# Four-head score pieces in the context attention of a two-layer decoder kernel

## The chip, the cores and the metric

The kernel runs on one core of a Trainium2 chip. The metric is the device time of one execution in microseconds (us), from its start to its end, as the median of several executions. The profile records one execution with a start and an end for every instruction. Its span runs from the first recorded instruction to the last.

## What is computed

The reference is a pre-norm decoder over x of shape (32, 112, 256), with two layers of causal attention, attention over a context and a mixture of experts. The change touches only the context attention of the second layer, which is cut here to what matters:

```
xn = layernorm(x)                       # 32 batches, 112 rows, 256 wide
q = rope(heads(xn @ Wq))                # 16 heads of 16
k = rope(heads(ctx @ Wk))               # ctx: 375 rows of a batch
v = heads(ctx @ Wv)
p = softmax(q @ k.T / 4)                # per head 112 x 375
x = x + (p @ v) @ Wo + bo
```

## The kernel before

**Stages.** The kernel runs its phases one after another. The context attention (class ContextAttention, from L1916, run by `stream`, L699) is one of them: in the trace its score matmuls run from 1754 us to 2398 us. It is one software pipeline over frames. In frame e every named piece works on batch e minus its age, so that one frame holds work of up to six batches. With 32 batches and ages of 0 to 5 there are 37 frames, and in 27 of them (5 to 31) every piece is present. The order of the pieces in a frame is one list written by hand (L1924), and all engines walk it in this order, each doing its part of a piece. Each engine works strictly in this order, so an engine that waits holds up all that it has behind the waiting piece. The trip through the frames is unrolled by 12.

**PSUM.** Six of the eight banks hold scores, as three pairs, 0, 1 and 2. The other two form a ring (class Ring, L226): each piece that isn't in the `bankless` list claims the next of the two in turn, and TensorE waits in `claim` until the piece that used this bank two claims earlier has been emptied by its reader.

**The pieces of one batch.** `stats` and `scale` normalise x on VectorE, with one power on GpSimd in between. `ctx0`, `ctx1` and `xT` transpose the context and x on TensorE, and ScalarE copies each out of its ring bank. `q`, `k0` and `k1` project, and ScalarE copies the results to `kq_raw`. Behind the last of the three in the frame's order ScalarE issues two transfers that exchange the halves of the partitions (`exchange`, L2151, to `kq_swapped`). `rope` on VectorE is three operations of 128x974 (L2207, L2210, L2211), the second of which waits for the exchange. Then 16 transfers issued by SyncE (`place_half`, L1992) spread the result to `slots`: each head lies in a 32-row slot, four heads side by side on the 128 partitions, four such groups g. `v0` to `v2` project the values.

**The scores.** A score piece is made for one group g and one half of its four heads: `g0` to `g3` for the first two heads, `h0` to `h3` for the other two. TensorE runs two matmuls of 32x112 by 32x375, each on its own 32 rows of the array and into its own bank of one pair (L2036; the trace records two instructions for each fp32 matmul, so x4 is one piece of two heads). VectorE takes the maximum over the 375 columns of both banks in one operation (L2194). After the last maximum VectorE writes the negative maxima to `top_wide` (L2203); `put` transposes them on TensorE (L2043), and VectorE adds them to q (L2215), so that the scores that are made a second time, transposed, come out with the maximum taken off. `tr0` to `tr2` (L2056) make these: sixteen matmuls of 32x125 by 32x112 each, on four row groups, into four banks (two pairs). One exponential of 125x1792 on ScalarE (L2141) empties them. `headsA` and `headsB` (L2095) multiply by the values, `back0`, `back1` (L2104) transpose back, VectorE divides (L2222, L2225), `onT` (L2111) transposes, `project` (L1563) projects and VectorE adds to x (L1587).

**Which pair serves which piece** is `first_pair` (L1932). `bank_free` (L2162) makes TensorE wait, before it writes a pair, for the reader of the piece that used it last: the maximum for a `g` or `h` piece, the exponential for a `tr` piece. The old order:

```
h0 g0 headsB tr0 g1 q back0 tr1 k1 k0 stats scale back1 h1 g2 onT rope
v0 ctx0 tr2 v1 xT h2 g3 h3 ctx1 headsA v2 project put
```

rope, stats and scale have no part on TensorE. `Ring.filled` and `Ring.freed` count the banks, and `copy_out` (L929) is the ScalarE copy whose line in the trace is L932.

Of the kernel before, what the change touches and what calls it, by code (L numbers as in the profile page):

```python
# [27 lines left out]
ALU = mybir.AluOpType  # L28
# [3 lines left out]
T = 112  # L32
# [7 lines left out]
S2 = 375  # L40
# [1875 lines left out]
class ContextAttention(Streamed):  # L1916
# [4 lines left out]

    def __init__(self, nc, G, W):
        super().__init__(nc, G, W)
        self.plan = Flow(2, [("h0", 3), ("g0", 3), ("headsB", 5), ("tr0", 4), ("g1", 3), ("q", 1), ("back0", 5),  # L1924
# [3 lines left out]
                             ("project", 5), ("put", 3)],  # L1928
                         bankless=("tr0", "tr1", "tr2", "g0", "h0", "g1", "h1", "g2", "h2", "g3", "h3", "rope", "stats", "scale"),
                         ahead=8, behind=5, turns=3, unroll=12)  # L1930

        self.first_pair = {"g0": 0, "g1": 0, "g2": 2, "g3": 1, "h0": 1, "h1": 0, "h2": 2, "h3": 0,  # L1932
                           "tr0": 1, "tr1": 0, "tr2": 0}
        names = [name for name in self.plan.names if name in self.first_pair]
        self.score_names = names
        self.last_maximum = [name for name in names if name[0] in "gh"][-1]
        self.last_raw = [name for name in self.plan.names if name in ("q", "k0", "k1")][-1]

    def allocate(self, sb, sem):
        self.norm = self.allocate_norm(sb, sem)  # L1940
        self.allocate_end(sb, sem)
        N = self.plan.turns
        self.ctx = self.G["contexts"]
        self.ctxT = [sb(f"ctxT{i}", [P, DC, S2]) for i in range(N)]
        self.xn, self.xT = sb("xn", [P, D]), sb("xT", [P, DC, T])
        self.kq_raw, self.kq_swapped = sb("kq_raw", [P, DC, KQ]), sb("kq_swapped", [P, DC, KQ])
        self.kq_part, self.kq = sb("kq_part", [P, DC, KQ]), sb("kq", [P, DC, KQ])
        self.slots = [sb(f"slots{i}", [P, HG, KQ]) for i in range(N)]
# [7 lines left out]
        self.scored, self.maxed = [sem(f"scored{i}") for i in range(2)], [sem(f"maxed{i}") for i in range(2)]  # L1956
# [66 lines left out]
    def pe(self, pe, name, b, par, c, body):  # L2023
        nc, ring, W = self.nc, self.ring, self.W
        slots = self.slots[par]
        if name in ("g0", "g1", "g2", "g3", "h0", "h1", "h2", "h3"):

            g, half = int(name[1]), "gh".index(name[0])
            if name == self.score_names[[n[0] in "gh" for n in self.score_names].index(True)]:
                pe.wait_ge(self.slotted, 256 * (b + 1))  # L2030
                self.tiles_set_up(pe, b)
            self.bank_free(pe, name, b)
            for a in range(2 * half, 2 * half + 2):
                slot = slice(SLOT * a, SLOT * (a + 1))
                at = 512 * (2 * self.first_pair[name] + a % 2)
                ins = nc.tensor.matmul(self.scores[0:T, at:at + S2], slots[slot, g, S2:KQ], slots[slot, g, 0:S2],  # L2036
                                       start=True, stop=True)
            ins.then_inc(self.scored[half], 1)
        elif name == "put":
            bank = ring.claim(pe, c, body)  # L2040
            pe.wait_ge(self.wide_ready, b + 1)
# [4 lines left out]
        elif name[0:2] == "tr":  # L2046
# [5 lines left out]
            for g in range(HG):  # L2052
                for a in range(HS):
                    slot = slice(SLOT * a, SLOT * (a + 1))
                    at = 512 * (2 * self.first_pair[name] + a) + g * T
# [62 lines left out]
    def act(self, act, name, b, par, c, body):  # L2118
        if name in ("ctx0", "ctx1"):
            self.copy_out(act, c, body, self.ctxT[par][:, int(name[3]), :], lambda bank: bank[:, 0:S2])  # L2120
        elif name == "xT":
            self.copy_out(act, c, body, self.xT[:].rearrange("p f t -> p (f t)"), lambda bank: bank[:, 0:DC * T])
        elif name == "q":
            at_least(act, self.turned, b)
            self.copy_out(act, c, body, self.kq_raw[:, :, S2:KQ], lambda bank: bank[:, 0:DC * T].rearrange("p (g t) -> p g t", g=DC))
            self.exchange(act, name, b)
        elif name in ("k0", "k1"):
            at_least(act, self.turned, b)
            self.copy_out(act, c, body, self.kq_raw[:, int(name[1]), 0:S2], lambda bank: bank[:, 0:S2])
            self.exchange(act, name, b)  # L2130
        elif name in ("v0", "v1", "v2"):
            self.tiles_set_up(act, b)
            self.copy_out(act, c, body, self.v[par][0:CK, int(name[1]), :, 0:HD],
                          lambda bank: bank[0:CK, 0:D].rearrange("t (h d) -> t h d", h=H))
        elif name[0:2] == "tr":
            i = int(name[2])
            act.wait_ge(self.flipped_ready, b * CC + i + 1)
            if i == 0:
                self.reuse(act, "headsB", b)
            at = 1024 * self.first_pair[name]  # L2140
            self.nc.scalar.activation(self.probsT[0:CK, i, :, :],  # L2141
                                      self.scores[0:CK, at:at + 2048].rearrange("t (a c) -> t a c", c=512)[:, :, 0:HG * T], ACT.Exp,
                                      scale=self.scale).then_inc(self.exped, 1)
        elif name in ("headsA", "headsB"):
            first = 0 if name == "headsA" else 2
            self.reuse(act, "back1" if first else "back0", b)
            self.copy_out(act, c, body, self.heads_raw[:, first * T:(first + 2) * T], lambda bank: bank[:, 0:2 * T])
        elif name == "onT":
            self.act_onT(act, b, c, body)
# [8 lines left out]
    def pairs_of(self, name):  # L2158
        first = self.first_pair[name]
        return {first, first + 1} if name[0] == "t" else {first}  # L2160

    def bank_free(self, pe, name, b):  # L2162
        names, age = self.score_names, self.plan.age
        here = names.index(name)
        waits = {}
        for pair in self.pairs_of(name):
            for back in range(1, 2 * len(names)):
                frame, at = divmod(here - back, len(names))
                other = names[at]
                if pair not in self.pairs_of(other):  # L2170
# [4 lines left out]
                i = int(other[-1])  # L2175
                sem, per = (self.exped, CC) if other[0] == "t" else (self.maxed["gh".index(other[0])], HG)
                waits[other] = (sem, before * per + i + 1)
                break
        for sem, count in waits.values():
            pe.wait_ge(sem, count)  # L2180
# [1 line left out]
    def dve(self, dve, name, b, par, c, body, chain):  # L2182
# [3 lines left out]
        elif name == "scale":  # L2186
            self.reuse(dve, "xT", b)
            self.norm_scale(dve, self.norm, b, self.xn[0:T, :], X[0:T, b, :]).then_inc(self.xn_ready, 1)
            nc.vector.tensor_tensor(X[0:T, b, :], X[0:T, b, :], self.W["cb"][0:T, :], ALU.add).then_inc(self.x_biased, 1)
        elif name in ("g0", "g1", "g2", "g3", "h0", "h1", "h2", "h3"):  # L2190
            g, half = int(name[1]), "gh".index(name[0])
            dve.wait_ge(self.scored[half], b * HG + g + 1)
            at = 1024 * self.first_pair[name]
# [1193 lines left out]
```

## Time and profile before

| | |
|---|---|
| median of 3 executions | 3161.06 us (3157.9 to 3165.23) |
| the profiled execution | 3160.0 us |
| its span | 3158.1 us |
| TensorE busy | 2782.6 us, 88% |
| VectorE busy | 2276.4 us, 72% |
| ScalarE busy | 1662.1 us, 53% |
| GpSimd busy | 961.8 us, 30% |
| mean granted TensorE clock | 0.939 |

PE is TensorE's matmuls, PEld its weight loads (which overlap them), DVE is VectorE, ACT ScalarE, POOL GpSimd and SP SyncE. The share of busy time is over the whole span; what counts for a change in one phase is the state of the engines in that phase. A clock of 1.00 is the upper of TensorE's two levels, 2.4 GHz, and 0.50 the lower, 1.2 GHz.

### The profile page before, as it was taken

What the parts mean: (1) busy time and instruction counts of PE and PEld (TensorE: products, weight loads), DVE (VectorE), ACT (ScalarE), POOL (GpSimd) and SP (SyncE); (2) the same over time, 40 slices, a digit from 0 to 9 for tenths busy, and PEclk for the clock granted to TensorE, in tenths of its full rate; (3) what the DMA queues carried; (4) which work ended last, traced back from release to release, by engine and by line L of the source; (5) the groups of instructions that cost most, each with busy time, mean ns of one, the idle gap of its engine ahead of it and who ended that gap; (6) DMA issues with size and microseconds to landing.
All of it is one profiled execution on the core that took longest, in us unless ns stands there. A gap on an engine that the chain in (4) does not pass through costs nothing. (4 is left out here: it accounts for less than half of the span.)

```text
span 3158.1 us, 76055 instructions
## 1 busy us (share of the span) xinstructions
PE 2782.6 (88%) x28240; PEld 2034.1 (64%) x28240; DVE 2276.4 (72%) x4894; ACT 1662.1 (53%) x3243; POOL 961.8 (30%) x1219
## 2 busy tenths in 40 slices
PE   7999899999999999667998799999997999983980
PEld 6887466666666665555886466666665777763970
DVE  5998567777777776567887577767763899984756
ACT  4777455655655555343554244444443788862540
POOL 0000344554555555460000100000000134546771
PEclk9999999999999999688999799999997999996995
DMA  7930354455445444262000333333330777857758
GB/s 179 300 92 0 109 158 141 132 162 162 139 146 165 150 132 152 86 203 72 0 0 7 63 71 71 72 71 72 72 62 22 232 230 231 247 173 219 225 173 249
DMA packets 364789, 413.72 MB, mean 131 GB/s; under 512 B 108017, under 2 KB 330513, under 8 KB 364369
## 3 DMA queue, kind: packets, MB, share of 16 engines
q1 hardware_dynamic: 218176, 220.63, 26.1%
q10 hardware_dynamic: 127216, 139.94, 15.1%
q0 software_dynamic: 19104, 49.22, 4.5%
q8 instruction: 189, 3.10, 0.4%
q14 instruction: 104, 0.84, 0.1%
HBM read 125.33 MB, written 252.45 MB: 120 GB/s over the span
## 5 line engine op out<-in xcount | busy, mean ns | idle before, releaser
L814 POOL TENSOR_TENSOR x_rstd<-x_var,g_minus_half 112x1 f32<-112x1 f32 x128 | 74.8, 585 | 710.5 <-DVE x_var L810 709.9
L2194 DVE TENSOR_REDUCE x_top<-x_scores 112x2 f32<-112x750 f32 x256 | 228.2, 933 | 78.7 <-PE x_scores L2036 76.2
L1369 ACT ACTIVATE x_probs<-x_held,x_minus_top 112x488 f32<-112x488 f32 x256 | 177.7, 697 | 173.4 <-DVE x_minus_top L1425 173.4
L1242 POOL TENSOR_TENSOR x_probs<-x_probs,x_inverse 112x488 f32<-112x488 f32 x256 | 250.7, 1000 | 10.2
L1283 PE MATMUL x_ring<-w_xkv,x_kv 128*122 128x512 f32 x512 | 236.3, 594 | 0.0
L1276 PE MATMUL x_ring<-x_kv,w_xkv 128*128 128x488 f32 x512 | 232.7, 587 | 1.1 <-ACT x_kv L1345 1.1
L932 ACT ACTIVATE x_v<-x_ring 122x512 f32<-122x512 f32 (+1 forms) x224 | 113.1, 505 | 182.5 <-PE x_ring L1283 151.9
L2141 ACT ACTIVATE x_probsT<-x_scores 125x1792 f32<-125x1792 f32 x96 | 159.8, 1665 | 83.3 <-PE x_scores L2056 83.3
L1419 DVE SCALAR_TENSOR_TENSOR x_held<-x_scores,x_keep 112x976 f32<-112x976 f32 x128 | 150.3, 1174 | 74.1 <-PE x_scores L1296 51.7
L814 POOL TENSOR_TENSOR a_rstd<-a_var,g_minus_half 112x1 f32<-112x1 f32 x64 | 35.6, 557 | 537.8 <-DVE a_var L810 537.8
L1237 POOL TENSOR_TENSOR x_inverse<-x_sums,x_minus_one 112x2 f32<-112x2 f32 x128 | 89.7, 701 | 226.9 <-ACT x_probs L1369 226.9
L3103 POOL DMA_INDIRECT expert_replies<-m_rows,m_reply_of x143 | 138.8, 970 | 55.9 <-issue 33.2
L1424 DVE TENSOR_REDUCE x_top<-x_held 112x2 f32<-112x976 f32 x128 | 149.8, 1170 | 4.4
L1283 PEld LDWEIGHTS x_ring<-w_xkv,x_kv 128*122 128x122 f32 x512 | 91.7, 185 | 94.8 <-issue 93.2
L2036 PE MATMUL x_scores<-x_slots 32*112 32x375 f32 x1024 | 137.0, 523 | 12.9 <-DMA x_slots<-x_kq 6.5
L1304 PEld LDWEIGHTS x_ring<-g_constants,x_probs 112*122 112x122 f32 x1024 | 109.9, 139 | 56.1 <-issue 51.4
L1276 PEld LDWEIGHTS x_ring<-x_kv,w_xkv 128*128 128x128 f32 x512 | 90.7, 192 | 79.7 <-issue 74.6
L932 ACT ACTIVATE x_probsT<-x_ring 122x448 f32<-122x448 f32 x256 | 130.6, 540 | 3.1 <-PE x_ring L1304 3.1
L1304 PE MATMUL x_ring<-g_constants,x_probs 112*122 112x112 f32 x1024 | 126.7, 260 | 3.6 <-POOL x_probs L1242 2.6
L1321 PEld LDWEIGHTS x_ring<-x_probsT,x_v 122*64 122x64 f32 x2048 | 99.1, 137 | 47.2 <-issue 46.1
L2313 POOL DMA_INDIRECT expert_slots<-r_rows,d_slot_of x96 | 99.3, 1035 | 95.1 <-ACT r_by_position L2614 64.4
L1296 PE MATMUL x_scores<-x_k,x_q 64*112 64x488 f32 x512 | 122.4, 596 | 3.2 <-DVE x_held L1419 3.2
(472 smaller groups left out, 7391.6 us busy)
## 6 DMA issues: line engine op xcount, KB each, us to landing
expert_slots<-d_empty ACTq DMA_DIRECT2D x32, 3612.0 KB, 16.8
by_position<-r_by_position SPq DMA_DIRECT2D x64, 784.0 KB
first_slots<-d_empty SPq DMA_DIRECT2D x8, 3612.0 KB, 32.6
r_bias<-by_position SPq DMA_DIRECT2D x64, 392.0 KB
m_rows<-expert_slots SPq DMA_DIRECT2D x143, 129.0 KB, 2.4
x_kq_swapped<-x_kq_raw ACTq DMA_DIRECT2D x64, 243.5 KB, 3.5
x_slots<-x_kq SPq DMA_DIRECT2D x512, 30.4 KB
m_rows<-expert_replies SPq DMA_DIRECT2D x32, 448.0 KB, 9.2
```

The lines of the kernel that those rows point to most:

```text
L932: self.ring.freed(self.nc.scalar.activation(dst, src_of(bank), ACT.Copy), c)
L1242: self.nc.gpsimd.tensor_tensor(probs, probs, self.inverse[0:T, u:u + 1].to_broadcast([T, XK]), ALU.mult).then_inc(self.weighted, 1)
L1276: ins = nc.tensor.matmul(bank[:, 0:XK], W["xkv"][:, f, m * P:(m + 1) * P], self.kv[:, f, :], start=(f == 0), stop=(f == DC - 1))
L1283: ins = nc.tensor.matmul(bank[0:XCK, :], self.kv[:, f, i * XCK:(i + 1) * XCK], W["xkv"][:, f, 512:1024], start=(f == 0), stop=(f == DC - 1))
L1304: ins = nc.tensor.transpose(bank[0:XCK, i * T:(i + 1) * T], self.probs[u % 6][0:T, i * XCK:(i + 1) * XCK], self.const("ident", T)[:, 0:T])
L1369: nc.scalar.activation(self.probs[u % 6][0:T, :], self.held[m % 2][0:T, i, :], ACT.Exp, scale=self.scale, bias=self.minus_top[0:T, m % 2, ...
L1419: nc.vector.scalar_tensor_tensor(self.held[m % 2][0:T, :, :], self.scores[0:T, 1024 * (m % 2):1024 * (m % 2 + 1)].rearrange("t (i c) -> t ...
L1424: chain.link(nc.vector.tensor_reduce(self.top[0:T, m % 2, :], self.held[m % 2][0:T, :, :], AX_X, ALU.max))
L2036: ins = nc.tensor.matmul(self.scores[0:T, at:at + S2], slots[slot, g, S2:KQ], slots[slot, g, 0:S2], start=True, stop=True)
L2141: self.nc.scalar.activation(self.probsT[0:CK, i, :, :], self.scores[0:CK, at:at + 2048].rearrange("t (a c) -> t a c", c=512)[:, :, 0:HG * ...
L2194: nc.vector.tensor_reduce(self.top[0:T, g, 2 * half:2 * half + 2], self.scores[0:T, at:at + 1024].rearrange("t (a c) -> t a c", c=512)[:, ...
L3103: pool.indirect_dma_start(replies[:, :], bass.IndirectOffsetOnAxis(reply_of[:, j:j + 1], 0), rows[:, R + j % R, 0:D], None).then_inc(repli ...
```

## The change

The eight score pieces of two heads become four pieces of four heads, `s0` to `s3`. TensorE makes the four matmuls of a group one after another, on the four row groups, into the four banks of two pairs, and signals once behind the last. VectorE takes the maxima in two operations, one for each pair, as large as before, and frees each pair on its own. `s0`, `s1` and `s2` write pairs 1 and 2, `s3` pairs 1 and 0, and all three `tr` pieces write pairs 0 and 1. The list of the frame is written anew: `k0` moves ahead of `back0`, and `q` and `k1` apart from it; `stats` moves ahead of `s1`; `scale` stays ahead of `back1`; `v0` stands ahead of `rope`; `onT` moves behind `v1`, `ctx0` behind `onT`, `v2` ahead of `xT`, and no score piece lies behind `xT` any more. The ages are the same. `k1` is now the last of q, k0 and k1, so the exchange is issued behind it.

```diff
-        self.plan = Flow(2, [("h0", 3), ("g0", 3), ("headsB", 5), ("tr0", 4), ("g1", 3), ("q", 1), ("back0", 5),
-                             ("tr1", 4), ("k1", 1), ("k0", 1), ("stats", 0), ("scale", 0), ("back1", 5), ("h1", 3),
-                             ("g2", 3), ("onT", 5), ("rope", 1), ("v0", 2), ("ctx0", 0), ("tr2", 4), ("v1", 2),
-                             ("xT", 0), ("h2", 3), ("g3", 3), ("h3", 3), ("ctx1", 0), ("headsA", 4), ("v2", 2),
-                             ("project", 5), ("put", 3)],
+        self.plan = Flow(2, [("s0", 3), ("headsB", 5), ("tr0", 4), ("k0", 1), ("back0", 5), ("stats", 0), ("s1", 3),
+                             ("q", 1), ("tr1", 4), ("k1", 1), ("scale", 0), ("back1", 5), ("s2", 3), ("v0", 2), ("rope", 1),
+                             ("tr2", 4), ("v1", 2), ("onT", 5), ("ctx0", 0), ("s3", 3), ("v2", 2), ("xT", 0), ("ctx1", 0),
+                             ("headsA", 4), ("project", 5), ("put", 3)],
...
-        self.first_pair = {"g0": 0, "g1": 0, "g2": 2, "g3": 1, "h0": 1, "h1": 0, "h2": 2, "h3": 0,
-                           "tr0": 1, "tr1": 0, "tr2": 0}
...
+        self.pairs_of = {"s0": (1, 2), "tr0": (0, 1), "s1": (1, 2), "tr1": (0, 1), "s2": (1, 2), "tr2": (0, 1), "s3": (1, 0)}
...
             self.bank_free(pe, name, b)
-            for a in range(2 * half, 2 * half + 2):
+            for a in range(HS):
                 slot = slice(SLOT * a, SLOT * (a + 1))
-                at = 512 * (2 * self.first_pair[name] + a % 2)
+                at = 512 * (2 * self.pairs_of[name][a // 2] + a % 2)
...
-            ins.then_inc(self.scored[half], 1)
+            ins.then_inc(self.scored, 1)
...
-                sem, per = (self.exped, CC) if other[0] == "t" else (self.maxed["gh".index(other[0])], HG)
-                waits[other] = (sem, before * per + i + 1)
+                i, half = int(other[-1]), self.pairs_of[other].index(pair)
+                if other[0] == "t":
+                    waits[other] = (self.exped, before * CC + i + 1)
+                else:
+                    waits[other, half] = (self.maxed[half], before * HG + i + 1)
...
-            dve.wait_ge(self.scored[half], b * HG + g + 1)
-            at = 1024 * self.first_pair[name]
-            nc.vector.tensor_reduce(self.top[0:T, g, 2 * half:2 * half + 2],
-                                    self.scores[0:T, at:at + 1024].rearrange("t (a c) -> t a c", c=512)[:, :, 0:S2],
-                                    AX_X, ALU.max).then_inc(self.maxed[half], 1)
+            dve.wait_ge(self.scored, b * HG + g + 1)
+            for half in range(2):
+                at = 1024 * self.pairs_of[name][half]
+                nc.vector.tensor_reduce(self.top[0:T, g, 2 * half:2 * half + 2],
+                                        self.scores[0:T, at:at + 1024].rearrange("t (a c) -> t a c", c=512)[:, :, 0:S2],
+                                        AX_X, ALU.max).then_inc(self.maxed[half], 1)
```

## Rows read from the trace of the kernel before

**Rows 1.** Busy time in stretches: us, then PE, PEld, DVE, ACT, POOL, clock, DMA.

```profile
2000.00:2100.00 100.00, 98.67 (x1399) 68.09 (x1388) 71.29 (x117) 47.79 (x76) 2.75 (x5) 1.00 0.34 72
...
2370.00:2375.00 5.00, 3.59 (x39) 2.07 (x34) 1.44 (x4) 1.96 (x2) 0.00 (x0) 0.75 0.23 36
```

**Rows 2.** The line that closes each batch's maxima, min/median/max ns, first and last start.

```profile
L2203 DVE TENSOR_SCALAR x_top_wide<-x_top x32: 181/182/185, 1777.7 to 2400.8; 112x16 f32<-112x16 f32 x32
```

**Rows 3.** Timeline of PE, one frame: start, us, instructions merged by line.

```profile
2042.30 0.90 PE L2036 MATMUL x_scores<-x_slots 32*112 32x375 f32 x8
...
2044.41 1.14 PE L2056 MATMUL x_scores<-x_q,x_slots 32*125 32x112 f32 x32
2045.38 0.80 PE L2036 MATMUL x_scores<-x_slots 32*112 32x375 f32 x4
2046.10 1.15 PE L917 MATMUL x_ring<-x_xT,w_cq 128*128 128x112 f32 x8
2047.09 0.38 PE L2104 MATMUL x_ring<-g_constants,x_heads_raw 128*112 128x128 f32 x2
...
2048.47 2.79 PE L2078 MATMUL x_ring<-x_ctxT,w_ck 128*128 128x375 f32 x8
2051.10 0.38 PE L2104 MATMUL x_ring<-g_constants,x_heads_raw 128*112 128x128 f32 x2
2051.41 0.90 PE L2036 MATMUL x_scores<-x_slots 32*112 32x375 f32 x8
...
2052.49 1.04 PE L925 MATMUL x_ring<-w_cv,x_ctxT 128*125 128x256 f32 x4
2053.66 0.54 PE L2065 MATMUL x_ring<-g_constants,c_context 125*128 125x125 f32 x3
2054.12 1.14 PE L2056 MATMUL x_scores<-x_q,x_slots 32*125 32x112 f32 x32
2055.20 1.13 PE L925 MATMUL x_ring<-w_cv,x_ctxT 128*125 128x256 f32 x4
2056.16 0.36 PE L906 MATMUL x_ring<-g_constants,x_xn 112*128 112x112 f32 x2
2056.45 1.52 PE L2036 MATMUL x_scores<-x_slots 32*112 32x375 f32 x12
2057.89 0.54 PE L2065 MATMUL x_ring<-g_constants,c_context 125*128 125x125 f32 x3
...
2061.96 0.90 PE L2036 MATMUL x_scores<-x_slots 32*112 32x375 f32 x8
```

**Rows 4.** Timeline of PEld, the same frame, inside the three adjacent score pieces.

```profile
2057.05 0.30 PEld L2036 LDWEIGHTS x_scores<-x_slots 32*112 32x112 f32 x8 [0.33 <-ACT x_probsT L2141]
```

**Rows 5.** Timeline of ACT, the same frame.

```profile
2051.87 1.12 ACTq L2155 DMA_DIRECT2D x_kq_swapped<-x_kq_raw  x2
...
2055.33 1.67 ACT L2141 ACTIVATE x_probsT<-x_scores 125x1792 f32<-125x1792 f32 x1 [0.62 <-PE x_scores L2056]
2056.89 0.38 ACT L932 ACTIVATE x_v<-x_ring 125x256 f32<-125x256 f32 x1
```

**Rows 6.** Timeline of DVE, the same frame.

```profile
2043.23 1.78 DVE L2194 TENSOR_REDUCE x_top<-x_scores 112x2 f32<-112x750 f32 x2
...
2047.51 0.21 DVE L2222 RECIPROCAL x_head_sums<-x_ring 112x8 f32<-112x8 f32 x1 [0.34 <-PE x_ring L2104]
...
2048.81 0.15 DVE L810 TENSOR_SCALAR x_var<-x_mv 112x1 f32<-112x1 f32 x1
...
2056.05 1.17 DVE L2210 TENSOR_TENSOR x_kq<-x_kq_swapped,g_constants 128x974 f32<-128x974 f32 x1 [0.83 <-DMA x_kq_swapped<-x_kq_raw]
```

**Rows 7.** Timeline of PE while the pipeline fills: v1, then ctx1.

```profile
1747.14 1.13 PE L925 MATMUL x_ring<-w_cv,x_ctxT 128*125 128x256 f32 x4 [0.93 <-ACT x_v L932]
...
1748.80 0.54 PE L2065 MATMUL x_ring<-g_constants,c_context 125*128 125x125 f32 x3 [0.34 <-ACT x_v L932]
```

**Rows 8.** Timeline of the SyncE queue: the 16 issues of one placement.

```profile
2058.58 11.63 SPq L1997 DMA_DIRECT2D x_slots<-x_kq  x16
```

More of the change, by code:

```diff
@@ L1923, in __init__ @@
         super().__init__(nc, G, W)
-        self.plan = Flow(2, [("h0", 3), ("g0", 3), ("headsB", 5), ("tr0", 4), ("g1", 3), ("q", 1), ("back0", 5),
[3 rows of a table removed]
-                             ("project", 5), ("put", 3)],
-                         bankless=("tr0", "tr1", "tr2", "g0", "h0", "g1", "h1", "g2", "h2", "g3", "h3", "rope", "stats", "scale"),
-                         ahead=8, behind=5, turns=3, unroll=12)
-        self.first_pair = {"g0": 0, "g1": 0, "g2": 2, "g3": 1, "h0": 1, "h1": 0, "h2": 2, "h3": 0,
-                           "tr0": 1, "tr1": 0, "tr2": 0}
-        names = [name for name in self.plan.names if name in self.first_pair]
-        self.score_names = names
-        self.last_maximum = [name for name in names if name[0] in "gh"][-1]
+        self.plan = Flow(2, [("s0", 3), ("headsB", 5), ("tr0", 4), ("k0", 1), ("back0", 5), ("stats", 0), ("s1", 3),
+                             ("q", 1), ("tr1", 4), ("k1", 1), ("scale", 0), ("back1", 5), ("s2", 3), ("v0", 2), ("rope", 1),
+                             ("tr2", 4), ("v1", 2), ("onT", 5), ("ctx0", 0), ("s3", 3), ("v2", 2), ("xT", 0), ("ctx1", 0),
+                             ("headsA", 4), ("project", 5), ("put", 3)],
+                         bankless=("tr0", "tr1", "tr2", "s0", "s1", "s2", "s3", "rope", "stats", "scale"),
+                         ahead=8, behind=5, turns=3, unroll=12)
+        self.pairs_of = {"s0": (1, 2), "tr0": (0, 1), "s1": (1, 2), "tr1": (0, 1), "s2": (1, 2), "tr2": (0, 1), "s3": (1, 0)}
+        self.score_names = [name for name in self.plan.names if name in self.pairs_of]
+        self.last_maximum = [name for name in self.score_names if name[0] == "s"][-1]
         self.last_raw = [name for name in self.plan.names if name in ("q", "k0", "k1")][-1]
@@ L1955, in allocate @@
         self.wide_ready = sem("wide_ready")
-        self.scored, self.maxed = [sem(f"scored{i}") for i in range(2)], [sem(f"maxed{i}") for i in range(2)]
+        self.scored, self.maxed = sem("scored"), [sem(f"maxed{i}") for i in range(2)]
         self.flipped_ready, self.exped = sem("flipped_ready"), sem("exped")
@@ L2025, in pe @@
         slots = self.slots[par]
-        if name in ("g0", "g1", "g2", "g3", "h0", "h1", "h2", "h3"):
-            g, half = int(name[1]), "gh".index(name[0])
-            if name == self.score_names[[n[0] in "gh" for n in self.score_names].index(True)]:
+        if name in ("s0", "s1", "s2", "s3"):
+            g = int(name[1])
+            if g == 0:
                 pe.wait_ge(self.slotted, 256 * (b + 1))
@@ L2054, in pe @@
                     slot = slice(SLOT * a, SLOT * (a + 1))
-                    at = 512 * (2 * self.first_pair[name] + a) + g * T
+                    at = 512 * (2 * self.pairs_of[name][0] + a) + g * T
                     ins = nc.tensor.matmul(self.scores[0:CK, at:at + T],
@@ L2139, in act @@
                 self.reuse(act, "headsB", b)
-            at = 1024 * self.first_pair[name]
+            at = 1024 * self.pairs_of[name][0]
             self.nc.scalar.activation(self.probsT[0:CK, i, :, :],
@@ L2156, in exchange @@
                               self.kq_raw[64 * (1 - i):64 * (2 - i), :, :]).then_inc(self.swapped, 16)
-    def pairs_of(self, name):
-        first = self.first_pair[name]
-        return {first, first + 1} if name[0] == "t" else {first}
     def bank_free(self, pe, name, b):
@@ L2165, in bank_free @@
         waits = {}
-        for pair in self.pairs_of(name):
+        for pair in self.pairs_of[name]:
             for back in range(1, 2 * len(names)):
@@ L2169, in bank_free @@
                 other = names[at]
-                if pair not in self.pairs_of(other):
+                if pair not in self.pairs_of[other]:
                     continue
@@ L2174, in bank_free @@
                     continue
-                i = int(other[-1])
-                sem, per = (self.exped, CC) if other[0] == "t" else (self.maxed["gh".index(other[0])], HG)
-                waits[other] = (sem, before * per + i + 1)
+                i, half = int(other[-1]), self.pairs_of[other].index(pair)
[3 more added lines that the diff above has]
+                    waits[other, half] = (self.maxed[half], before * HG + i + 1)
                 break
@@ L2189, in dve @@
             nc.vector.tensor_tensor(X[0:T, b, :], X[0:T, b, :], self.W["cb"][0:T, :], ALU.add).then_inc(self.x_biased, 1)
-        elif name in ("g0", "g1", "g2", "g3", "h0", "h1", "h2", "h3"):
-            g, half = int(name[1]), "gh".index(name[0])
-            dve.wait_ge(self.scored[half], b * HG + g + 1)
-            at = 1024 * self.first_pair[name]
-            nc.vector.tensor_reduce(self.top[0:T, g, 2 * half:2 * half + 2],
-                                    self.scores[0:T, at:at + 1024].rearrange("t (a c) -> t a c", c=512)[:, :, 0:S2],
-                                    AX_X, ALU.max).then_inc(self.maxed[half], 1)
+        elif name in ("s0", "s1", "s2", "s3"):
+            g = int(name[1])
+            dve.wait_ge(self.scored, b * HG + g + 1)
[4 more added lines that the diff above has]
+                                        AX_X, ALU.max).then_inc(self.maxed[half], 1)
             if name == self.last_maximum:
```

## The prediction

> **What bounds the kernel now.** I first cut the time into stretches. The phase that is changed fills the span from 1754 to about 2400 us, and in its middle TensorE is busy 98.67 us of 100 at a granted clock of 1.00, VectorE 71 and ScalarE 48 [rows 1]. So TensorE's row of matmuls is the phase: what it saves, or any time that it waits, is the time of the kernel. The next phase starts behind it. Then I looked for the length of a frame: the score pieces h0, g0 start at 2042.30 and again at 2061.96, so an undisturbed frame is 19.66 us [rows 3]. The line that closes a batch's maxima runs 32 times from 1777.7 to 2400.8, which is 20.10 us a frame in the mean [rows 2]; the 0.44 on top are late transfers and the emptier frames at the end. Last I read the timeline of one frame on each engine. In rows that are merged by line, the distance from one start to the next is what a piece costs TensorE; a duration overlaps with its neighbour.
>
> **What the pieces cost.** A piece of two heads alone, g1, takes 0.72 (2045.38 to 2046.10). Four heads side by side take 0.84: the x8 loads of g3, h3 start at 2057.05 and the next piece at 2057.89 [rows 3, 4]. So two more heads on the other row groups cost 0.12. The four places of scores in the frame are 0.84, 0.72, 0.84 and 1.44 (2056.45 to 2057.89), 3.84 in all; four pieces of four heads are 4 x 0.84 = 3.36. **The packing saves 0.48 a frame.** VectorE's work doesn't change: eight maxima, two in 1.78 [rows 6], so I take 0.93 for the first, with its signal 0.05 later. Two small things move with it. v0 to ctx0 took 1.17 where v1 to xT took 0.96, since ctx0 waited for the bank of onT: 0.21 that goes with the old order. And a tr piece in front of full-array work takes 1.08 (2054.12 to 2055.20) against 0.97 in front of a score piece: tr0 now stands before k0, 0.10 more. The bare new frame is 19.66 - 0.48 - 0.21 + 0.10 = 19.07.
>
> **What waits in the new order.** tr and s pieces now share pair 1 every time, and s1, s2 can't start before the exponential of the tr before them, nor tr before the maxima of the s before it. I lay the new order out, with s0 at 0, from the distances of the rows.
> - tr0 starts at 2.11 as now (2042.30 to 2044.41, s0 and headsB) [rows 3]. The first maximum starts 0.93 behind s0 (2043.23) [rows 6] and its pair is free at 1.91: no wait, 0.20 to spare.
> - s1 needs exponential 0. It starts 1.21 behind its tr, takes 1.67 [rows 5] and frees the pair 0.05 later (57.00 to 57.05 [rows 4]): 2.93 behind tr0, at 5.04. TensorE has only tr0 1.07, k0 1.32 (half of 2048.47 to 2051.10) and back0 0.31 in between, and is there at 4.81. **Wait 0.24.**
> - tr1 needs the first maximum of s1. In VectorE's queue back0 and stats now stand before it. back0's reciprocal starts 0.42 behind its matmuls and the variance ends 1.45 behind the reciprocal (2047.51 to 2048.96) [rows 3, 6]: 4.50 + 0.42 + 1.45 = 6.37, where the scores lie ready at 5.97. Pair 1 is free at 6.37 + 0.93 + 0.05 = 7.35. TensorE is there at 5.04 + 0.84 + 0.99 (q) = 6.87. **Wait 0.48.**
> - s2 needs exponential 1: 7.35 + 2.93 = 10.28, while tr1, k1, back1 end at 10.05. **Wait 0.24.**
> - tr2 needs the first maximum of s2: 10.28 + 0.93 + 0.93 + 0.05 = 12.19, TensorE comes at 10.28 + 0.84 + 0.96 = 12.08. **Wait 0.11.**
> - ctx0 claims the bank that v1 filled, and ScalarE copies v1 behind exponential 2. In the rows this copy starts 2.77 behind tr2 (2054.12 to 2056.89) and takes 0.38 [rows 3, 5]; with a signal of 0.05 to 0.12 the bank is free 3.22 behind tr2, at 15.41. TensorE has tr2 1.08, v1 0.96, onT 0.29 (as xT) and is there at 14.52. **Wait 0.89.** In the old frame xT and three score pieces stood behind v1, and hid this copy. Behind the waiting ctx0 stand s3 and all the rest of the frame.
> - s3 at 15.87 finds exponential 2 over. v2 at 16.71, xT at 17.67.
> - ctx1 claims the bank of v2. The rows of the fill show this pattern, a v piece, xT, then ctx1: 1.66 from start to start, with ScalarE's copy named [rows 7]. So ctx1 at 18.37 where TensorE comes at 17.96. **Wait 0.41.**
> - From ctx1 to the next s0 it is 2057.89 to 2061.96, 4.07, less the v2 that has moved, 0.96: 3.11 [rows 3]. **The frame is 21.48 us.**
>
> The six waits are 2.37 a frame and eat the 0.59 that was saved three times over.
>
> **What is moved and costs nothing.** The exchange is issued behind k1's copy, about 10.7 into the frame where it was 9.57 (2051.87). It landed some 4.2 behind its issue (2056.05) [rows 5, 6], so rope ends near 17.3. Then two maxima, 1.8, and top_wide, 0.2: 19.3, while put stands at 21.0. So put, which sometimes waited for top_wide, has 1.7 us of cover; without this cover each us of late exchange would cost one. ScalarE's queue holds nothing but copies behind its two issues. SyncE's 16 issues take 11.6 [rows 8], start at 17.5 instead of 16.3 and end in the next frame at 7.6, before rope writes again at 15 and more than a frame before s0 needs them. Its context load waits for ctx0 and has a frame to land. GpSimd has one power; scale, which needs it, now stands behind the two maxima of s1, and xT in the same frame stands far behind. One signal for four heads costs at most what a lone half gained, nothing, since g0 and h0 ended together.
>
> **The sum.** 21.48 - 19.66 = 1.82 a frame undisturbed. In the mean frame the waits of put for top_wide go, and some of the late transfers fall into waits that are there anyhow; I take 0.2 of the 0.44 off: 1.6. All pieces meet in 27 frames, and one frame while it fills has the same waits: 28 x 1.6 = 45. In the last frames q, k and ctx are missing and TensorE waits for the exponentials in either order; by the same laying out I get one frame 0.5 shorter and one up to 2 shorter, and put this at 0 for want of rows at the slower clock. Against the profiled execution's 3160.0 us this gives 3205; the median of the three is 1 us above it: **3206 us**, 1.4% slower. Bounds of the case: signals of 0.05 or of 0.12 and a copy that overlaps move the six waits by about 0.3 in all either way, and if the late transfers stay in full or go in full the frame moves by 0.25: 28 x 0.55 = 15, and 6 more below if the last frames gain: 3185 to 3222.
>
> What ScalarE and VectorE do to the banks is also a rule of the Trainium skill (TensorEngine Tiling (Array Packing), section PSUM Bottleneck): packing speeds up TensorE but not the emptying of PSUM, which may become the bottleneck. It gives no time; the waits above say the same of this kernel.
>
> **Rivals.**
> - *The waits are covered and the packing is kept* (faster). Place: ctx0 and tr1. If v1's bank and pair 1 came free in time, and the others with them, the frame would be 19.07 against a mean of 20.10: 28 x 1.0 = 28 less, 3133. It decides below 1.0 us of waits a frame. For it: VectorE has 29% free and ScalarE 52% [rows 1]. Against: the two longest, 0.89 and 0.48, come from the order of one queue, and are 1.37 by themselves.
> - *The clock falls.* Now TensorE hardly rests. In the new frame it rests 1.30 of the 3.85 us before ctx1. In 2370 to 2375, where it was busy 3.59 of 5, the granted clock was 0.75, so it stood at the lower level, 1.2 GHz, for half of this stretch [rows 1]. If it fell in every frame for some 4 us of work, these would take 2 more: 28 x 2 = 56 on top, 3260. Against: over a whole frame of the new order the busy share is 19.1 of 21.5, 89%. The skill has a case of this (TensorE: Matmul & The Clock Gate, section on psum-queue depth-cycling): short rests at each bank in turn let the clock swing; no steady stretch here shows it.
> - *Only the ring waits count*: the short waits of 0.11 to 0.48 don't come, as the exponential or the maxima start earlier than I have it. Then 1.30 of waits, 20.37, less than 1 above now: 28 x 0.5 = 14, 3175.
>
> **How the numbers follow.** Forecast 0.77, falling clock 0.09, ring waits alone 0.07, covered 0.07. The range must leave out no more than 0.2: from 3184 to 3236, which holds the first case with both its bounds and a clock that falls in one frame of two or three, and leaves out 3260 and most of the last two. A measurement of this kernel tells 0.2%, 6 us, from no change. Faster by more: the covered case, 0.07. Within: part of the third, 0.03. Slower: 0.90.
>
> **What would show it.** Right: in the waits, s1 and s2 after L2141's exponential with 0.2 to 0.3 each, a tr piece after L2194's maximum, and L2065 held up by ScalarE's copies twice a frame; starts of the first score piece 21.5 us apart; TensorE busy near 90% in this phase. Wrong: a frame under 20.1, no gap ahead of ctx0, a granted clock under 1.00 in the steady part, or put waiting for top_wide again.

## The result, and the profile after

The changed kernel took 3203.05 us (median of 4, 3198.01 to 3210.36) where the kernel before took 3162.4 (median of 4). The ratio is 1.0142, with a 95% interval of 1.0127 to 1.0158; the quotient of the two medians alone is 1.0129. 3206 had been forecast. Measured again on another chip (e5 below) it was 1.0152 (1.0129 to 1.0176).

The profiled execution took 3210.36 us, with a span of 3208.6. This is one frame of the changed kernel on TensorE, from the timeline (start, us, instructions merged by line; in square brackets the idle time before them and what ended it):

```profile
2040.23 0.90 PE L2033 MATMUL x_scores<-x_slots 32*112 32x375 f32 x8
...
2044.78 0.38 PE L2101 MATMUL x_ring<-g_constants,x_heads_raw 128*112 128x128 f32 x2
2045.27 0.90 PE L2033 MATMUL x_scores<-x_slots 32*112 32x375 f32 x8
2046.10 1.15 PE L917 MATMUL x_ring<-x_xT,w_cq 128*128 128x112 f32 x8
2047.60 1.14 PE L2053 MATMUL x_scores<-x_q,x_slots 32*125 32x112 f32 x32 [0.35 <-DVE x_top L2190]
...
2050.03 0.38 PE L2101 MATMUL x_ring<-g_constants,x_heads_raw 128*112 128x128 f32 x2
2050.52 0.90 PE L2033 MATMUL x_scores<-x_slots 32*112 32x375 f32 x8
2051.35 1.13 PE L925 MATMUL x_ring<-w_cv,x_ctxT 128*125 128x256 f32 x4
2052.48 1.14 PE L2053 MATMUL x_scores<-x_q,x_slots 32*125 32x112 f32 x32
...
2054.52 0.36 PE L2108 MATMUL x_ring<-g_constants,x_normed 112*128 112x112 f32 x2
2055.76 0.54 PE L2062 MATMUL x_ring<-g_constants,c_context 125*128 125x125 f32 x3 [0.88 <-ACT x_v L932]
...
2058.02 0.36 PE L906 MATMUL x_ring<-g_constants,x_xn 112*128 112x112 f32 x2
2058.65 0.54 PE L2062 MATMUL x_ring<-g_constants,c_context 125*128 125x125 f32 x3 [0.28 <-ACT x_v L932]
...
2061.84 0.90 PE L2033 MATMUL x_scores<-x_slots 32*112 32x375 f32 x8
```

They answer to [rows 3]. The frame is 21.61 us, where it was 19.66. A short wait does not show as idle time of PE, because the rows of matmuls overlap; it shows in the distance between starts. back0 costs 0.31 and starts at 2044.78, so s1 could start at 2045.09 and starts at 2045.27.

| wait of TensorE | forecast | measured | how it is read |
|---|---|---|---|
| s1, for exponential 0 | 0.24 | 0.18 | 2045.27 - (2044.78 + 0.31) |
| tr1, for the first maximum of s1 | 0.48 | 0.51 | 2047.60 - (2046.10 + 0.99) |
| s2, for exponential 1 | 0.24 | 0.18 | 2050.52 - (2050.03 + 0.31) |
| tr2, for the first maximum of s2 | 0.11 | 0.17 | 2052.48 - (2051.35 + 0.96) |
| ctx0, for the copy of v1 | 0.89 | 0.95 | 2055.76 - (2054.52 + 0.29) |
| ctx1, for the copy of v2 | 0.41 | 0.34 | 2058.65 - (2058.02 + 0.29) |
| sum | 2.37 | 2.33 | |

In the weight loads of the same frame the causes have names (timeline of PEld):

```profile
2045.27 0.29 PEld L2033 LDWEIGHTS x_scores<-x_slots 32*112 32x112 f32 x8 [0.35 <-ACT x_probsT L2138]
...
2050.52 0.29 PEld L2033 LDWEIGHTS x_scores<-x_slots 32*112 32x112 f32 x8 [0.35 <-ACT x_probsT L2138]
```

And this is why tr1 waited: VectorE had the scores of s1 ready at 2046.2, but took them behind the statistics (timeline of DVE, answering to [rows 6]):

```profile
2045.20 0.21 DVE L2218 RECIPROCAL x_head_sums<-x_ring 112x8 f32<-112x8 f32 x1 [2.22 <-PE x_ring L2101]
...
2046.51 0.15 DVE L810 TENSOR_SCALAR x_var<-x_mv 112x1 f32<-112x1 f32 x1
2046.60 1.78 DVE L2190 TENSOR_REDUCE x_top<-x_scores 112x2 f32<-112x750 f32 x2
```

In the stretch of this frame (columns as in [rows 1]) TensorE is busy 19.88 of 21.61 us, at a granted clock of 1.00:

```profile
2040.23:2061.84 21.61, 19.88 (x275) 13.40 (x274) 13.97 (x24) 9.32 (x15) 0.55 (x1) 1.00 0.29 64
```

**The account of the two profiled executions.** The piece `put` marks the end of a frame. Before, it runs at 1803.36, at the end of the last frame that isn't full yet, and at 2344.22, 27 frames later; the next phase's first transpose is at 2434.66:

```profile
1803.36 0.57 PE L2043 MATMUL x_ring<-g_constants,x_top_wide 112*128 112x112 f32 x4 [1.50 <-DVE x_top_wide L2203]
...
2344.22 0.55 PE L2043 MATMUL x_ring<-g_constants,x_top_wide 112*128 112x112 f32 x4
...
2434.66 0.64 PE L906 MATMUL r_ring<-g_constants,r_xn 112*128 112x112 f32 x2 [5.56 <-DVE r_xn L2639]
```

After:

```profile
1801.95 0.60 PE L2040 MATMUL x_ring<-g_constants,x_top_wide 112*128 112x112 f32 x4 [0.48 <-ACT x_heads_raw L932]
...
2390.59 0.55 PE L2040 MATMUL x_ring<-g_constants,x_top_wide 112*128 112x112 f32 x4
...
2484.97 0.63 PE L906 MATMUL r_ring<-g_constants,r_xn 112*128 112x112 f32 x2 [5.57 <-DVE r_xn L2635]
```

27 frames take 588.64 us instead of 540.86, 47.8 more or 1.77 a frame. The last frames and the start of the next phase take 94.4 instead of 90.4, 3.9 more. Up to the put of 1803.36 it is 1.4 less, 1.0 of it in the last frame of the filling. That is 50.3 of the 50.5 by which the spans differ. The mean frame is 21.80: of the 0.19 over 21.61 nearly all is one late transfer of slots in the middle (one frame of 26.55), which the kernel before has as well (one of 24.78). In none of the 27 frames does put wait for top_wide any more.

### The profile page after: what moved, and what is told of

Same layout as the page of the kernel before. It is cut to its first block and busy times, and to the rows that moved or that the text cites. A ratio compares the mean times of both kernels' runs of the same rounds, so it can differ in the third digit from the quotient of the medians.

```text
span 3208.6 us, 76120 instructions
## 1 busy us (share of the span) xinstructions
PE 2789.2 (87%) x28240; PEld 2031.1 (63%) x28240; DVE 2270.7 (71%) x4894; ACT 1656.0 (52%) x3243; POOL 962.4 (30%) x1219
## 5 line engine op out<-in xcount | busy, mean ns | idle before, releaser
L1276 PEld LDWEIGHTS x_ring<-x_kv,w_xkv 128*128 128x128 f32 x512 | 90.4, 191 | 79.3 <-issue 74.3
L2033 PE MATMUL x_scores<-x_slots 32*112 32x375 f32 x1024 | 119.0, 535 | 21.2 <-ACT x_probsT L2138 7.8
L2053 PE MATMUL x_scores<-x_q,x_slots 32*125 32x112 f32 x3072 | 114.6, 287 | 17.9 <-DVE x_top L2190 14.4
```

The source lines that it names most:

```text
L1276: ins = nc.tensor.matmul(bank[:, 0:XK], W["xkv"][:, f, m * P:(m + 1) * P], self.kv[:, f, :], start=(f == 0), stop=(f == DC - 1))
```

## The experiments

The theory is that of the prediction: the time of this phase is TensorE's row of matmuls, 19.1 us a frame, plus the waits that the order of three queues and the pairs make, and each wait is set by the piece that its reader has ahead of it. The rivals: the ring waits alone count; the four-head piece itself costs, since it needs two pairs at once; the new order costs and the pieces gain; the clock. Four kernels ran on one chip (before 3152.63 there), four on a second (before 3159.08), three on a third (before 3159.95).

**e1, statistics behind s1.**

```diff
-... ("back0", 5), ("stats", 0), ("s1", 3), ("q", 1), ...
+... ("back0", 5), ("s1", 3), ("stats", 0), ("q", 1), ...
```

> The changed kernel with one move in the list: stats stands behind s1, so that VectorE takes the maxima of s1 before the statistics. Theory (the frame is TensorE's row plus the waits that the order of the queues makes): the maxima of s1 start 0.93 us behind s1 instead of 1.33, tr1 starts some 0.4 us earlier (its wait falls from 0.5 to about 0.1) and everything behind it moves with it; frame 21.61 to 21.2, and 28 x 0.4 = 11 us less than the changed kernel, 3192. Rival A (only the two waits for ScalarE's copies of v set the frame, and what is saved ahead is waited for there): frame 21.6, 3203. Rival B (the scale step, which needs GpSimd's power behind the statistics, becomes late): frame above 21.6.

Measured: 3199.28 us, ratio 1.0148 (1.013 to 1.0165). The frame is 21.25 (2036.68 to 2057.93), 0.36 less, and tr1 starts 1.13 behind q where it was 1.50:

```profile
2036.68 0.90 PE L2033 MATMUL x_scores<-x_slots 32*112 32x375 f32 x8
...
2042.55 1.15 PE L917 MATMUL x_ring<-x_xT,w_cq 128*128 128x112 f32 x8
2043.68 1.14 PE L2053 MATMUL x_scores<-x_q,x_slots 32*125 32x112 f32 x32
...
2057.93 0.90 PE L2033 MATMUL x_scores<-x_slots 32*112 32x375 f32 x8
```

The frame says that tr1's wait was the statistics' place, and that nothing behind it in the frame takes the gain back; rivals A and B fall. The total doesn't show it: 3192 had been expected, and the ratio, 1.0148, is not under that of the changed kernel, 1.0142 and 1.0152 on other chips. In the traces the 27 full frames take 580.6 us where the changed kernel takes 588.6, and the last frames 1.0 more. What takes the gain back in the medians is not found; the chip is one candidate.

**e2, v1 ahead of tr2.**

```diff
-... ("v0", 2), ("rope", 1), ("tr2", 4), ("v1", 2), ("onT", 5), ...
+... ("v0", 2), ("rope", 1), ("v1", 2), ("tr2", 4), ("onT", 5), ...
```

> The changed kernel with v1 ahead of tr2, so that ScalarE copies v1 before the exponential of tr2, and ctx0 finds its bank free. Theory: the wait of 0.9 in front of ctx0 goes and does not come off the frame: tr2 starts about 0.8 later, its exponential ends 0.8 later, and s3, which shares pairs 0 and 1 with tr2, waits some 1.1 for it. Frame 21.6 within 0.1, time 3203 within 6, a new wait of s3 for the exponential. Rival A (the ring alone is the cost): frame 20.7, 3178.

Measured: 3208.1 us, ratio 1.0171 (1.0153 to 1.0188), frame 21.59. ctx0 follows onT after 0.24, and s3 waits:

```profile
2055.64 0.41 PE L2108 MATMUL x_ring<-g_constants,x_normed 112*128 112x112 f32 x2
2055.88 0.49 PE L2062 MATMUL x_ring<-g_constants,c_context 125*128 125x125 f32 x3
2057.49 0.90 PE L2033 MATMUL x_scores<-x_slots 32*112 32x375 f32 x8 [1.12 <-ACT x_probsT L2138]
```

The longest wait was removed, and came back at the next piece, longer, for the same exponential. So the 0.95 in front of ctx0 was not the price of the ring of two banks alone: a second limit, the pair that s3 needs, lay right behind the first.

**e3, half an exponential.** Each exponential takes half of its columns, 125x896 instead of 125x1792, and the other half of the probabilities is left at a constant. So half of this work is left out.

> The changed kernel with each exponential over half of its columns (125x896 instead of 125x1792; the other half of the probabilities is a constant, so half of the exponentials are left out). The exponential falls from 1.67 to about 0.92 us. Theory: the waits of s1 and s2 for it (0.18 each) go, and the wait of ctx0, whose copy stands behind exponential 2, falls from 0.9 to about 0.2; the wait of tr1 for the maxima of s1 stays or grows by 0.2, as it doesn't hang on the exponential. Frame 20.7, 28 x 0.9 = 26 less, 3177. Rival A (ring alone, not the exponential ahead of the copy): ctx0's wait stays at 0.9, frame 21.2. Rival C (VectorE's maxima or the exchange bound the frame): frame 21.4 or more.

Measured: 3170.61 us, ratio 1.0053 (1.0036 to 1.007), frame 20.92 (2030.14 to 2051.06). The rows of the wait that fell and of the one that didn't:

```profile
2037.52 1.14 PE L2054 MATMUL x_scores<-x_q,x_slots 32*125 32x112 f32 x32 [0.53 <-DVE x_top L2191]
...
2044.97 0.54 PE L2063 MATMUL x_ring<-g_constants,c_context 125*128 125x125 f32 x3 [0.36 <-ACT x_v L932]
```

s1 now follows back0 after 0.31, without a wait, and tr1 waits 0.69 (1.68 behind q) instead of 0.51: it hangs on VectorE, as said. ctx0's idle time falls from 0.88 to 0.36 and no further. The frame fell by 0.69, not 0.9; in the timeline of ScalarE the copy of v1 starts at 2044.46, where the exponential (0.92, from 2043.43) would let it start at 2044.25, since v1 itself runs from 2043.29 to 2044.42. With the shorter exponential the matmuls of v1 are the limit. By the ratios the total fell by some 30 us, more than the 28 x 0.69 = 19 of these frames. The traces say where the rest is: from the last full frame to the next phase it is 80.1 us (2370.81 to 2450.92) instead of 94.4, 14.3 less. The last frames wait longest for exponentials.

**e4, the pieces alone, in the old order.** List: s0 headsB tr0 s1 q back0 tr1 k1 k0 stats scale back1 s2 onT rope v0 ctx0 tr2 v1 xT s3 ctx1 headsA v2 project put; s0, s1, s2 on pairs (0, 2), s3 on (0, 1), tr on (0, 1).

> The pieces alone: the order of the kernel before, with each group of two-head pieces replaced by one piece of four heads (s0 for h0 g0, s1 for g1, s2 for h1 g2, s3 for h2 g3 h3), on pairs 0 and 2 (s3 on 0 and 1), tr pieces on 0 and 1. Theory: s1 directly behind tr0 finds only pair 2 free and waits some 2.0 us for exponential 0, s3 waits 0.6 for exponential 2, and the other waits are small; frame 21.5 to 21.7, about 3200: it is the four-head piece's need of two pairs at once that costs, and the new order spreads the same cost. Rival D (the new order is what costs, and the pieces by themselves gain): frame 19.2 to 19.5, 3150.

Measured: 3239.97 us, ratio 1.0277 (1.0259 to 1.0295): a miss by 40 us in the total. The waits are there nearly as laid out, 1.78 of idle time before s1 (2.0 expected) and 0.53 before s3 (0.6). Of the 26 full frames without the late transfer, 8 are 21.6 to 21.7 and 18 are 23.2 or more. The difference is in the rows behind s1, here of two frames with the same wait:

```profile
1990.01 0.90 PE L2033 MATMUL x_scores<-x_slots 32*112 32x375 f32 x8 [1.78 <-ACT x_probsT L2138]
1990.84 1.15 PE L917 MATMUL x_ring<-x_xT,w_cq 128*128 128x112 f32 x8
1991.82 0.38 PE L2101 MATMUL x_ring<-g_constants,x_heads_raw 128*112 128x128 f32 x2
1992.13 1.14 PE L2053 MATMUL x_scores<-x_q,x_slots 32*125 32x112 f32 x32
...
2035.59 0.90 PE L2033 MATMUL x_scores<-x_slots 32*112 32x375 f32 x8 [1.78 <-ACT x_probsT L2138]
2036.42 1.87 PE L917 MATMUL x_ring<-x_xT,w_cq 128*128 128x112 f32 x8
2038.09 0.63 PE L2101 MATMUL x_ring<-g_constants,x_heads_raw 128*112 128x128 f32 x2
2038.65 1.79 PE L2053 MATMUL x_scores<-x_q,x_slots 32*125 32x112 f32 x32
```

The stretches before and behind the start of the second s1, with the granted clock in the third column from the end:

```profile
2030.00:2035.50 5.50, 3.81 (x94) 2.70 (x92) 2.83 (x4) 1.98 (x2) 0.00 (x0) 1.00 0.31 47
2035.50:2042.00 6.50, 6.41 (x55) 4.84 (x56) 3.70 (x9) 1.88 (x3) 0.55 (x1) 0.74 0.17 27
```

Behind the second wait q, back0 and tr1 take 1.67, 0.56 and 1.72 from start to start instead of 0.98, 0.31 and 1.07: 1.6 us lost, part of the stretch at 1.2 GHz (a mean clock of 0.74). So the rival of the falling clock is real, in another order than the one it was weighed for. The 18 slow frames account for 29 of the 40 us; the rest was not taken apart. Without the fall the frame is what the theory gave, and rival D (the pieces gain, the new order costs) falls.

**e10, the same with q ahead of s1,** to tell the clock from a wrong sum.

```diff
-... ("tr0", 4), ("s1", 3), ("q", 1), ("back0", 5), ...
+... ("tr0", 4), ("q", 1), ("s1", 3), ("back0", 5), ...
```

> The four-head pieces in the old order, as before (frame 23.3), with one move: q stands ahead of s1, so that it lies inside s1's wait for exponential 0. Two theories of the 23.3. Clock: the wait of 1.78 in one piece made the granted clock fall for some 6 us in every frame (1.6 us lost in each); with q inside, the longest wait is 0.9, the clock stays at 1.00, and the frame is 21.3, 3200. Waits alone (the laid-out sum was simply wrong by 1.6): the frame falls by at most the 0.99 of q, to 22.3 or more, with the granted clock still under 1.00 behind s1.

Measured: 3212.89 us, ratio 1.017 (1.0149 to 1.0192), 27 us under e4. The frame is 21.55 (2040.80 to 2062.35), and only three of 26 are 23.2 to 23.3. The stretch that has s1, back0 and tr1 in it:

```profile
2045.80:2052.00 6.20, 5.46 (x56) 3.32 (x60) 3.69 (x10) 2.57 (x4) 0.55 (x1) 1.00 0.20 31
```

The undisturbed frames hardly differ (21.7 and 21.55): the 0.99 of q that went into the wait came back, 0.70 of it as idle time of tr1 before a maximum. What the move gained is the clock. I had expected 21.3, and a fall in every frame of e4; it fell in 18 of 26.

**e5 and e6, the changed kernel again, and with v2 behind headsA.**

```diff
-... ("v2", 2), ("xT", 0), ("ctx1", 0), ("headsA", 4), ("project", 5), ...
+... ("xT", 0), ("ctx1", 0), ("headsA", 4), ("v2", 2), ("project", 5), ...
```

> The changed kernel once more, unedited, on the chip on which the other runs of this call stand, so that they can be compared with it directly. Frame 21.6, ratio to the kernel before 1.014 to 1.018.

> The changed kernel with v2 behind headsA, where the kernel before had it. Theory: ctx1 no longer claims the bank of v2 but that of s3's neighbour ctx0, emptied long before, so its wait of 0.34 goes, and project behind v2 costs 0.86 instead of 0.95; frame 21.61 to 21.2, 28 x 0.4 = 12 less than the changed kernel. Rival (the waits only move within the frame, as with v1 ahead of tr2): frame 21.6.

Measured: e5 3205.47 us, frame 21.62. e6 3209.33, ratio 1.0158 (1.0138 to 1.0177), frame 21.46: a miss, 0.15 less and not 0.4, and no gain in the total. In the traces the 27 full frames take 4.6 less than those of e5, while the last frames take 3.4 more, and this execution comes to the phase's first put 5.5 later. ctx1 follows xT after 0.24, as expected, but headsA now claims the bank of xT, and waits for its copy:

```profile
2037.02 0.49 PE L2062 MATMUL x_ring<-g_constants,c_context 125*128 125x125 f32 x3
2037.82 1.36 PE L2092 MATMUL x_ring<-x_probsT,x_v 125*32 125x112 f32 x48 [0.31 <-ACT x_xT L932]
```

I had looked at the claim of ctx1 and not at the next one. In the old order three score pieces stood between xT and ctx1.

**e9, one pair at a time.**

```diff
-            self.bank_free(pe, name, b)
-            for a in range(HS):
+            for half in (1, 0):
+                self.bank_free(pe, name, b, (self.pairs_of[name][half],))
+                for a in range(2 * half, 2 * half + 2):
...
-    def bank_free(self, pe, name, b):
+    def bank_free(self, pe, name, b, pairs=None):
...
-        for pair in self.pairs_of[name]:
+        for pair in pairs or self.pairs_of[name]:
```

> The changed kernel, but each s piece waits for one pair at a time: it waits for its second pair and makes the two heads of it, then waits for the first pair and makes the other two (row groups 2, 3, 0, 1); still one signal at the end. Theory: in s1 and s2 the first two heads run while the exponential still holds pair 1, so each ends 0.1 to 0.35 us earlier. For s1 nothing comes of it, since tr1 waits for VectorE, whose maxima of s1 start behind the statistics anyway; for s2 it does. Frame 21.3 to 21.5 against 21.6. Rival D3 (it is the need of both pairs at once that costs most of the loss): frame under 20.8.

Measured (one execution): 3202.4 us beside 3159.95, frame 21.59. A miss: next to nothing. s1 starts at 2045.42, directly behind back0 (2045.11), and so 0.18 earlier than it would, but takes 0.99 to the next piece instead of 0.83:

```profile
2045.11 0.38 PE L2102 MATMUL x_ring<-g_constants,x_heads_raw 128*112 128x128 f32 x2
2045.42 1.06 PE L2034 MATMUL x_scores<-x_slots 32*112 32x375 f32 x8
2046.41 1.15 PE L917 MATMUL x_ring<-x_xT,w_cq 128*128 128x112 f32 x8
```

The trace of the single matmuls shows why: the first two heads start at 2045.42, the other two, held by the exponential, at 2045.59, and from there it is 0.82 to q, as much as four heads take together and not the 0.72 of two heads alone. So the piece ends when it would have. Waiting for both pairs at once, and not for one after the other, costs nothing here, and D3 falls; that s1 needs the exponential's pair at all still costs its 0.18.

**e7, e8 and e11, four-head pieces in other orders.** The lists stand in the expectations.

> Four-head pieces in another order, laid out so that work that needs neither the banks of an exponential nor ScalarE stands behind each tr piece: s0 headsB s1 k1 tr0 k0 stats q back0 s2 v0 ctx0 tr1 back1 scale rope v1 onT tr2 project v2 s3 xT ctx1 headsA put, pairs s0 (2,0), s1 (1,2), s2 (2,0), s3 (2,0), tr0 (0,1), tr1 (1,2), tr2 (1,2). Theory: if the loss of the changed kernel is its order and pairs and not the four-head piece, the waits fall from 2.5 to about 0.6 a frame: frame 19.6, and without the waits for late exchanges that the kernel before has, a mean of 19.8: 2 to 8 us faster than the kernel before. Rival D2 (four heads at once need two pairs at once and can't be had cheaper): frame 20.5 or more, slower than before.

> As the last, with another order: s0 headsB tr0 stats k0 q back0 tr1 scale back1 k1 s1 v0 xT s2 onT ctx0 ctx1 tr2 rope v1 v2 s3 headsA project put, pairs s0 (1,2), s1 (1,0), s2 (1,2), s3 (0,2), all tr (0,1). k0 and q stand behind tr0, back1 and k1 behind tr1, v1 and v2 behind tr2, and s1 only after both. Theory: waits of about 0.6 a frame, frame 19.6 to 19.7, 2 to 8 us faster than the kernel before. Rival D2: frame 20.5 or more. Rival E (s1 and s2 near each other make VectorE's maxima late): tr2 waits for a maximum, frame 20.0 to 20.5.

> The second laid-out order with four-head pieces (frame 19.61, ratio 0.9962 in the first measurement) once more, in five rounds. If the gain is real: ratio 0.995 to 0.998 with an interval that leaves out 1. If it was luck of the executions: an interval that holds 1.

Measured: e7 3154.58 us, ratio 0.9982 (0.997 to 0.9994), frames of 19.9 to 20.1 and not 19.6; headsA waits 0.31 to 0.48 for the copy of xT, the same neighbour as in e6. e8 3145.88 us beside 3159.08, ratio 0.9962 (0.9948 to 0.9976), frame 19.61. e11, the same kernel on another chip: 3151.48 beside 3159.95, ratio 0.9971 (0.9958 to 0.9984). **This order of four-head pieces beats both kernels**, the one before by 0.3 to 0.4% and the changed one by some 1.8%. Its frame around the tr pieces, from the trace of e8:

```profile
2039.73 1.14 PE L2053 MATMUL x_scores<-x_q,x_slots 32*125 32x112 f32 x32
2040.80 1.53 PE L2075 MATMUL x_ring<-x_ctxT,w_ck 128*128 128x375 f32 x4
2042.16 1.04 PE L917 MATMUL x_ring<-x_xT,w_cq 128*128 128x112 f32 x8
2043.04 0.41 PE L2101 MATMUL x_ring<-g_constants,x_heads_raw 128*112 128x128 f32 x2
2043.38 1.14 PE L2053 MATMUL x_scores<-x_q,x_slots 32*125 32x112 f32 x32
...
2046.31 0.90 PE L2033 MATMUL x_scores<-x_slots 32*112 32x375 f32 x8 [0.16 <-ACT x_probsT L2138]
```

tr0 is followed by k0, q and back0 and then tr1, which reuses its pairs: 3.65 us of work where the exponential needs 2.93, and no score piece whose maxima could be late. Undisturbed, the frame is only 0.05 shorter than before, 1.4 in 27. In the profiled execution of e8 27 frames take 535.7 us (put from 1801.38 to 2337.11) instead of 540.9, so 3.8 more come from waits that are gone, put's for late exchanges above all, and the phase enters them 2.0 earlier. Between e8 and the changed kernel several moves lie at once, so that the pair tells what an order is worth, and not which move.

## Why the prediction was right

**The bound.** TensorE's row was the phase, before and after: 19.28 of matmuls and 2.33 of waits are the frame of 21.61, and in e1 a wait that got 0.37 shorter made the frame 0.36 shorter.

**The packing.** A four-head piece costs 0.83 from start to start (2045.27 to 2046.10), 0.84 had been taken, and two of the old places cost 0.83 too (2042.30 to 2043.13). That is a gain of 0.50 a frame, 3.32 for 3.82. Even e8 doesn't keep it: its other pieces cost 0.45 more than before (k0 and k1 with the wait of s1 behind them 0.32, project 0.20, the two ctx pieces 0.15, tr0 0.10, against 0.21 less for v0 and 0.11 less for q).

**The six waits.** All six are there, each for the cause named, none off by more than 0.07, sum 2.33 for 2.37. Of the causes, e1 shows the one of tr1, e3 that of s1 and s2 and over half of ctx0's (0.52 of idle time); e6 that ctx1's hangs on what stands around it. That of tr2 is read from the trace alone.

**What was mis-sized.** The frame came out 21.61 and not 21.48. The bare frame, 19.07, was 0.2 short (19.11 by the layout, 21.48 less 2.37: the two sums don't quite meet): k0 and k1, which had been adjacent, cost 1.37 and 1.36 alone, not 1.32, and project 0.95 behind headsA, not the 0.86 that it cost behind v2, which the step "From ctx1 to the next s0" had taken over. The 0.2 that was taken off for vanishing waits in the mean frame was right in kind: it was 20.03 - 19.66 = 0.37 before and 0.19 after. The 28th frame, the last of the filling, was to lose 1.6 like the others; it gained 1.0 (24.27 instead of 25.29), and all that lies ahead of the full frames 1.4. The last frames, put at 0, cost 3.9: the rows of the end show waits of 1.42, 1.15 and 1.16 in one frame, and behind the first of them slower pieces, tr1 1.48 and s2 1.54 from start to start where they take 1.07 and 0.83 in the full frames. I had laid them out at full clock and seen a gain.

```profile
2415.70 0.90 PE L2033 MATMUL x_scores<-x_slots 32*112 32x375 f32 x8 [1.42 <-ACT x_probsT L2138]
2417.76 1.55 PE L2053 MATMUL x_scores<-x_q,x_slots 32*125 32x112 f32 x32 [1.15 <-DVE x_top L2190]
...
2421.07 1.61 PE L2033 MATMUL x_scores<-x_slots 32*112 32x375 f32 x8 [1.16 <-ACT x_probsT L2138]
```

**Where it was luck.** The mechanism was right, but that 3206 lies within 3 us of 3203 is in part luck. The profiled pair differs by 50.4 us and the medians by 41 (46 in e5), where 45 had been added; the full frames cost 4.6 more than the sum had it, the end 3.9 more, and what lies ahead of them 3.0 less (1.6 had been added there, and 1.4 was gained). Two slips in the arithmetic changed nothing: the waits are four times the 0.59 and not three, and 56 on 3206 is 3262.

**The rivals.** *The waits are covered*: it fell by its own point, 2.33 against 1.0. In another order the waits can be nearly covered, as e8 shows, though its frame is 19.61 and not 19.07. *Only the ring waits count*: fell; the four short waits came, 1.04 in all, and e2 removes the longer ring wait without any gain. *The clock falls*: not in the undisturbed frames of the changed kernel, granted clock 1.00 with waits up to 0.95. It did in the one frame with the late transfer, where TensorE stands idle for 3.29 and the clock is 0.66 in the 5 us behind (2130 to 2135). In e4, with one of 1.78, it fell in most of them.

The rule of the Trainium skill that stood beside the sum (TensorEngine Tiling (Array Packing), section PSUM Bottleneck) is borne out in kind: every one of the six waits is for an engine that empties PSUM. But VectorE and ScalarE were busy 65% and 43% of the frame. Their speed counts where a wait hangs on it (e3, 0.69 a frame); the order of the same pieces counts for more (e8, 2.0 a frame).

## What to carry to other kernels

When pieces are merged that hold a buffer, look at each buffer's next writer and at what stands between the two: here a pair comes free 2.93 us behind the start of the matmuls of a tr piece, and 1.9 behind the start of a score piece, and the order must put that much independent work there. Lay out the whole frame, claim by claim, since the next limit can lie a few tenths behind the first: a wait that was removed alone gave all of itself in e1, less than half in e6 and nothing in e2. Where a bank's copy stands behind a long instruction in its reader's queue, as v1's does behind an exponential, put work that needs no ring bank ahead of the piece that claims this bank next; in the old order xT and three score pieces stood there.

## What was not expected of the hardware

- **The clock falls after one longer wait, in some frames and not in others.** A wait of 1.78 us in a frame that is otherwise nearly full cost 1.6 us of slower matmuls behind it, in 18 frames of 26 (23.3 against 21.7 us); with idle times of 0.71 and 0.70 close together it happened in three of 26 (a mean clock of 0.76 in 1981 to 1988 of e10). The changed kernel's 0.88 and e2's 1.12 did it in none of their undisturbed frames. Why one frame has it and the next doesn't is open.
- **Half a piece first is no gain.** With two heads 0.17 us ahead of the other two the piece is 0.99 long instead of 0.83, and the later two take 0.82 where two heads alone take 0.72 (e9).
- **Neighbours change the price of a piece by 4 to 10%.** project costs 0.86 behind v2 and 0.95 behind headsA, and 0.87 when e6 puts v2 ahead of it again; k0 and k1 cost 2.63 together and 2.73 apart. In the timeline of the weight loads project's first load starts 0.22 ahead of its first matmul behind v2 (2060.40 and 2060.62, before) and together with it behind headsA (2060.41, after).
